# A transformer layer on one core: the last product moved into the next batch's slots, and the counting pass without its constant half

## The reference

```
x = L0_attn_x                                    # (16, 512, 256)
Q, K, V = heads(x @ Wq.T + bq), heads(x @ Wk.T + bk), heads(x @ Wv.T + bv)
scores = einsum('bhqd,bhkd->bhqk', Q, K) / 4     # (16, 16, 512, 512)
top_vals, _ = top_k(scores, 31)
scores = where(scores < top_vals[..., -1:], -inf, scores)
context = softmax(scores) @ V
x = layernorm(x + context @ Wo.T + bo)
gate, up = x @ (w_gate / 127).T, x @ (w_up / 127).T      # 768 hidden
x = layernorm(x + (silu(gate) * up) @ (w_down / 127).T)
```

## Time and profile before

| what | us |
|---|---|
| median of three runs (lowest, highest) | 2992.36 (2987.83, 2993.67) |
| the profiled execution's own time | 3002.92 |
| its span, from the first to the last instruction | 3001.1 |
| PE busy | 2705.3 (90%) |
| DVE, ACT, POOL busy | 2499.2, 2478.7, 2385.7 |
| mean granted TensorE clock | 0.959 of full speed |

### The profile page before, as it was taken

The page is one execution under the profiler, slowest core; times in us unless marked ns, Lnnn a source line. Parts: engine busy times, 40 slices in busy tenths (PEclk is TensorE's granted clock), DMA queues, the critical chain, the costliest instruction groups (busy, mean ns, idle before and its releaser), DMA issues.

```text
span 3001.1 us, 81706 instructions
## 1 busy us (share of the span) xinstructions
PE 2705.3 (90%) x21375; PEld 1449.9 (48%) x21375; DVE 2499.2 (83%) x12312; ACT 2478.7 (83%) x5890; POOL 2385.7 (79%) x1668
## 2 busy tenths in 40 slices
PE   5889999989998988899999999999988999899897
PEld 2444544545454444454545455454444545455455
DVE  5888888888889878888898988878888888888883
ACT  4888898888898877888888988878978888888883
POOL 1887888888798876787888888787877879778783
PEclk7899999999999989899999999999999999999998
DMA  3201111020111101111011110211101111110100
GB/s 88 48 21 42 25 41 38 24 49 26 37 30 36 42 21 37 29 29 45 23 42 25 41 39 24 47 27 37 30 25 45 26 40 27 32 42 23 37 2 22
DMA packets 91162, 102.67 MB, mean 34 GB/s; under 512 B 34529, under 2 KB 52962, under 8 KB 90594
## 3 DMA queue, kind: packets, MB, share of 16 engines
q1 hardware_dynamic: 89874, 96.35, 13.4%
q10 hardware_dynamic: 720, 0.14, 0.0%
HBM read 20.86 MB, written 8.39 MB: 10 GB/s over the span
## 4 chain that ended last, share of the span: by engine, by line
PE 36%; DVE 18%; SPq 15%; issue 13%; POOL 8%; ACT 6%; DMA 2%; DVEq 1%; ACTq 0%; POOLq 0%
SPq L386 8%; SPq L385 7%; DVE cand L941 7%; POOL mask L1219 6%; PE bench L740 5%; PE Y_ps L664 5%; PE ST_ps L684 4%; PE Y_ps L661 3%; PE ctxT_ps L698 3%; DVE S L934 3%; PE bench L734 3%; PE bench L605 3%; PE Y_ps L662 3%; PE ST_ps L681 3%; ACT junk L492 2%
## 5 line engine op out<-in xcount | busy, mean ns | idle before, releaser
L1219 POOL TENSOR_SCALAR mask<-S,thr,mb 128x512 bf16<-128x512 f32 x1015 | 2098.4, 2080 | 44.1 <-POOL mb L1213 33.5
L941 DVE MAX8 cand<-Y_ps 128x8 f32<-128x128 f32 x4096 | 1072.0, 282 | 7.4 <-issue 6.9
L492 ACT ACTIVATE junk<-S,at_zero,slope 128x512 bf16<-128x512 f32 x1024 | 824.7, 805 | 99.3 <-DVE S L934 99.2
L934 DVE TENSOR_SCALAR_CACHE_REDUCE S<-S_ps,na 128x512 f32<-128x512 f32 x1024 | 755.9, 738 | 170.7 <-PE S_ps L651 153.2
L502 ACT ACTIVATE above<-S,s,steep 128x512 bf16<-128x512 f32 x1024 | 824.6, 805 | 0.6
L510 ACT ACTIVATE PT<-ST_ps 128x512 f32<-128x512 f32 x1024 | 595.9, 582 | 193.0 <-PE ST_ps L684 187.4
L661 PE MATMUL Y_ps<-ones_b,nbig 128*128 128x512 bf16 x1024 | 403.0, 394 | 169.6 <-DVE cand L941 155.9
L651 PE MATMUL S_ps<-KS,QS 64*128 64x512 f32 x1024 | 523.0, 511 | 4.5 <-DVE S L934 2.3
L664 PE MATMUL Y_ps<-KS,QS 64*128 64x512 f32 x1024 | 523.0, 511 | 0.0
L684 PEld LDWEIGHTS ST_ps<-nbig,mask 128*128 128x128 bf16 x4096 | 235.8, 99 | 382.0 <-issue 382.0
L684 PE MATMUL ST_ps<-nbig,mask 128*128 128x128 bf16 x4096 | 414.8, 225 | 0.0
(11 more groups left out here) (187 smaller groups left out, 3684.6 us busy)
## 6 DMA issues: line engine op xcount, KB each, us to landing
QS<-Qhi SPq DMA_DIRECT2D x512, 32.0 KB, 2.0
KS<-Khi SPq DMA_DIRECT2D x512, 32.0 KB, 2.0
KS<-Klo SPq DMA_DIRECT2D x512, 32.0 KB, 2.0
QS<-Qlo SPq DMA_DIRECT2D x512, 32.0 KB, 2.0
xTs<-in_xT SPq DMA_DIRECT2D x17, 512.0 KB, 3.7
xs<-in_x SPq DMA_DIRECT2D x16, 512.0 KB, 3.9
out<-xs SPq DMA_DIRECT2D x15, 512.0 KB, 2.9
hT<-in_wgT SPq DMA_DIRECT2D x1, 768.0 KB
```

The source lines that it names most:

```text
L492: nc.scalar.activation(junk[:, :], S[:, score_place(j)[0], :], ACT.Tanh, bias=at_zero[:, :], scale=slope[:, hb, col:col + 1], accum_out=s0 ...
L934: nc.vector.tensor_scalar(S[:, at, :], S_ps[n % 2][:, :], na[:, hb, col:col + 1], None, ALU.add, op1=ALU.max, accum_out=rmax[:, n % RING:n ...
L941: mx = nc.vector.max(cand[:, j % CANDS, i, :], Y_ps[j % 2][:, i * BW:(i + 1) * BW])
L1219: nc.gpsimd.tensor_scalar(mask[:, h % MASKS, t, :], S[:, score_place(j)[0], :], thr[:, r:r + 1], mb[:, r:r + 1], ALU.is_lt, op1=ALU.add).t ...
```

## The change

Six things change together.

1. The four down products leave slots 59 to 62 and stand in slots 1, 2, 3 and 5 of the next batch, with DVE's sums and statistics one slot behind; the second layer norm is at slot 7 there, and the normalised rows at 10 and 12. Only batches from 2 on have them (`finish`), and the rest slots have the last ones.
2. Gate and up stand at 43/44, 46/47, 49/50, 52/53, 58/59 and 61/62. The products gram and quad go from 36 and 37 to 42 and 45, sums from 55 to 54.
3. `below` loses its constant product. ACT writes its Sign as one unsigned byte, the upper one of each bf16 of `above` (the lower stays 0): 1 gives 2^-125 and anything else 0. The weights are -2^127, so the product is 0 or -4. To match, W_k and b_k are multiplied by 2^-38 once, and the exponential's scale undoes it.
4. In 30 slots, the list `QUIET`, that product is made twice.
5. `flag` and `onesc` are bf16 (the small flag product is one pass, not two).
6. Batch 1 is written apart on all engines. The loops cover batches 2 to 15: seven batches per body on PE, ACT and POOL (one return, after batch 8), two on DVE (six returns, after batches 3, 5, 7, 9, 11 and 13).

```diff
-BIG = 2.0 ** 40
+SHIFT = 2.0 ** -38
+BIG = 4.0
+BYTE_BIG = 2.0 ** 127
...
-             26: "v", 31: "q", 33: "k", 35: "keys", 36: "gram", 37: "quad", 55: "sums"}
+             26: "v", 31: "q", 33: "k", 35: "keys", 42: "gram", 45: "quad", 54: "sums"}
...
-DOWN_SLOTS = {59: 0, 60: 1, 61: 2, 62: 3}
+DOWN_SLOTS = {1: 0, 2: 1, 3: 2, 5: 3}
...
-LN_SLOTS = {34: 0, 63: 1}
+LN1_SLOT, LN2_SLOT = 34, 7
...
-OUT_SLOTS = {1: (0, 1), 2: (2, 3)}
+OUT_SLOTS = {10: (0, 1), 12: (2, 3)}
...
-        if n in DOWN_SLOTS:
-            uses.append(("down", DOWN_SLOTS[n]))
+    if finish and n in DOWN_SLOTS:
+        uses.append(("down", DOWN_SLOTS[n]))
...
-TURN_OF, ACT_TURN_OF = 5, 7
+TURN_OF, DVE_TURN_OF = 7, 2
...
+QUIET = [n for n in range(TILES)
+         if all(what in ("flags", "keys", "gram", "quad") for what, _ in uses_of(n, False, False, True))]
...
-                nc.scalar.activation(above[:, j % 4, :], S[:, score_place(j)[0], :], ACT.Sign, bias=s0[:, j % 8:j % 8 + 1],
+                nc.scalar.activation(above[:, j % 4, :].bitcast(U8).rearrange("p (l y) -> p l y", y=2)[:, :, 1], S[:, score_place(j)[0], :], ACT.Sign, bias=s0[:, j % 8:j % 8 + 1],
...
-                nc.tensor.matmul(Y[:, :], nbig[:, :], ones_b[:, :], start=True, stop=False)
-                nc.tensor.matmul(Y[:, :], nbig[:, :], above[:, j % 4, :], start=False, stop=False)
+                for again in range(1 + (n in QUIET)):
+                    nc.tensor.matmul(Y[:, :], nbyte[:, :], above[:, j % 4, :], start=(again == 0), stop=False)
...
-                        pe.wait_ge(h_done, b * NF)
+                        pe.wait_ge(h_done, (b - 1) * NF)
                         mm = narrow(part)
...
-            with pe.Fori(1, B, TURN_OF) as b:
+            slots(1, False, False, False)
+            with pe.Fori(2, B, TURN_OF) as b:
                 for i in range(TURN_OF):
-                    slots(b + i, False, False)
-            slots(B, False, True)
+                    slots(b + i, False, False, True)
+            slots(B, False, True, True)
...
-            with dve.Fori(1, B, TURN_OF) as b:
-                for i in range(TURN_OF):
-                    slots(b + i, False, False)
-            slots(B, False, True)
+            slots(1, False, False, False)
+            with dve.Fori(2, B, DVE_TURN_OF) as b:
+                for i in range(DVE_TURN_OF):
+                    slots(b + i, False, False, True)
+            slots(B, False, True, True)
```

More of the change, by code:

```diff
@@ L742, in narrow, with on_bench @@
                 return mm
[L744 to L746 removed]
+            def on_bench(b, n, first, rest, finish):
+                for what, part in uses_of(n, first, rest, finish):
+                    use = place(b, n, what, part, first, rest, finish)
                     pe.wait_ge(taken, use)
```

116 lines of the change are left out of this document (62 added, 54 removed).

## The result

| | median of the runs, us | range | runs |
|---|---|---|---|
| before | 2992.21 | 2987.83 to 2993.67 | 4 |
| after | 3060.82 | 3056.57 to 3068.04 | 4 |

The ratio is 1.0234 with a 95% interval of [1.0208, 1.026]: the change makes the kernel 2.3% slower, about 70 us. The forecast was 3003 us with a range of 2955 to 3035. The direction was right, the size was not.

What follows compares the result with a forecast made beforehand. It took PE to bound slots 41 to 0 and ACT the light slots, with four engines close. Terms -153 + 120 + 10.8 - 4.5 + 30 + 8 = +11.3 gave 3003 us against the median, range 2955 to 3035.

Steps and rivals of the forecast that it cites:

- slots 41 to 0: Slot 41 to the next slot 0: bound goes from PE to ACT, 60.5 us, -10.2 each, -153 us in all.
- slots 1 to 5: Slots 1 to 5, batches 2 to 15: moved down products make them PE-bound at 19.9 us, +8.6 each, +120 us.
- rest slots: Rest slots after the last batch: its four down products find no cover on a busy PE, +10.8 us.
- slots 6 to 31: Slots 6 to 31: ten constant products go, but ACT and the load behind SP's issues hold the length, 0 us.
- slots 32 to 40: Slots 32 to 40: gram and quad leave while ACT is nearly full, -0.3 us each, -4.5 us.
- loop returns: DVE's loop returns, six instead of two: stall and half clock cost 7.6 us each, +30 us net.
- wait for the last hT: First down product in slot 1: PE waits for POOL's last hT, 1 us in eight batches, +8 us.
- the first rival: DVE's loop returns are cheap, one stop and no fall of the clock: -4 instead of +30, 2969 us; chance 0.22.
- The clock falls more often: PE with less work is granted half clock in more stretches: +50 us, or 3030 us if half count; chance 0.10.
- Everything comes through: ACT is not the bound, so the 7.5 us of constant products per batch are saved everywhere: 2925 us; chance 0.10.
- The late hT: PE stands in slot 1 for POOL's hT, 4 us in 14 batches: +48 at most, 3030 us; chance 0.16.

Runs made afterwards that it cites:

- b_down1: The kernel before with five of the six matmuls of each down product left out in the loop batches; 2931.97 us, ratio 0.9809.
- a_both7: The changed kernel with the fifth gate and up products at slots 59 and 60, sums at 51 and one DVE return; 3004.92 us, ratio 1.0051.
- b_bytes: The kernel before with the byte pass alone (no constant product, bf16 flags, W_k scaled), order and loops as before; 2992.84 us, ratio 1.0003.
- a_down_only: The changed kernel with gate, up, gram, quad and sums back in the slots of the kernel before; 3043.44 us, ratio 1.0162.
- a_gate59: The changed kernel with the fifth gate and up products one slot later (59 and 60), so slot 58 is free; 3036.94 us, ratio 1.0156.
- a_all_twice: The changed kernel with the byte product made twice in all 64 slots instead of 30; 3062.18 us, ratio 1.0234.
- b_bytes15: The kernel before with the byte pass alone and all fifteen batches in one loop body on PE, DVE and POOL; 2972.64 us, ratio 0.994.

## Why the prediction was wrong

Against the profiled execution, in us:

| term | forecast | measured | how |
|---|---|---|---|
| slots 41 to 0, without returns | -153 | -94 | -87.0, of which returns +7 |
| slots 1 to 5, without returns | +120 | +116 | +124.9, of which returns +9 |
| rest slots | +10.8 | +9.7 | what lies outside the batches' slots |
| slots 6 to 31 | 0 | -2 | table above |
| slots 32 to 40 | -4.5 | +8 | table above |
| loop returns | +30 | +16 | 6 x 5.3 less 16 |
| wait for the last hT | +8 | 0 | no such wait |
| sum | +11.3 | +53.7 | |

**The step that failed** is the first: "with short waits, as a near tie of three engines leaves them, I take 60.5 (ends 59.1 and 64). That is -10.2 each". Measured are 64.7 against 70.7, -6.0 each, outside even the upper end. This term alone is 59 us too low. The whole sum is only 42 short, since the other terms together were 17 us too high, the returns and the wait for hT above all: they hid part of the miss. ACT's busy time was right (59.05 forecast, 59.56 in batch 9). What failed is the step from a bound to a length. The runs show three things in its place:

- The bench wait of slot 58, an order effect that no busy time shows. Taking it away in two ways gave 23 and 30 us, some of it through the clock behind the returns. The forecast looked at what was removed from slots 59 to 62 and never asked what a product put into slot 58 would wait for: the bench's one bank, still holding the turned context.
- The down products were cover. Taking 132 us of them out of slots 59 to 62 saved 57 (`b_down1`). The forecast priced what leaves PE at its full length down to ACT's bound and called what stays short waits.
- ACT's bound is not reached. Even with both repairs (`a_both7`) slots 41 to 0 take 62.9 us by the medians, so that 1.8 of the 4.2 us by which 64.7 exceeds the forecast's 60.5 are gone and 2.4 stay; in batch 7 the stretch is 61.9 us with its fullest engine at 57.8, 93%. The light slots, where ACT was at 99 to 100%, were the wrong model for slots in which nearly every one has a product that passes over the bench. That it is the bench that makes the difference is likely from the waits above, and not shown: what holds these 2.4 us per batch stays open.

**Slots 1 to 5** were right: 20.2 us against a forecast of 19.9, PE full. So was the sentence that what was PE-bound with ACT idle stays so in another place; the stretches above are its measurement.

**Slots 32 to 40** went the other way, +8 for -4.5. Slots 38 to 40 grew, and nearly every batch after has a stretch at half clock from about slot 38 to 41, 3.4 to 13.7 us long. Over all batches slots 38 to 41 took 184 us before, 204 after, and 198 in `b_bytes`, so the byte pass alone can bring most of the growth. It does not always: `a_down_only` has it too, with gram and quad at 36 and 37 as before, and stands at 184. What else it takes is not shown.

**Loop returns** had the right mechanism and were mis-sized, 7.6 us each for 5.1 to 5.3. The stops are shorter (2.4 and 0.9 us for 3.3 and 1.8), as the first rival had said, though there are still two; the fall of the clock that it denied is there, 6.8 us after each. It costs 2.6 to 2.8 us in slots 1 to 5, where the forecast had 3.4. In `a_gate59`, without the wait of slot 58, the rival's price holds: no fall of the clock, and 1.8 to 2.6 us a return.

**The wait for the last hT** is absent: no row of PE's or PEld's waits names hT, and the down product in slot 1 starts straight behind the turned scores. POOL's side was right: the last hT of batch 8 is done 24.6 us after slot 57 begins (1643.29), 24 forecast.

```profile
1666.66 1.26 POOL L1272 TENSOR_TENSOR hT<-th,ups 128x512 f32<-128x512 f32 x1
```

PE's side was not: it reaches the down product at 1670.41, after 27.1 us and not 22 to 23, the wait of slot 58 among them.

**The rivals.** "The clock falls more often" was right as an observation (71 stretches for 36, 520 us for 250). As the cause of the 70 us it fails by `a_all_twice`, which is as slow with 285 us; behind the returns the fall does cost 2.6 to 2.8 us each. "Everything comes through" is refuted by `b_bytes`. The late hT did not occur. None of the rivals was an order effect on the bench. The range ended 26 us too low, since its slow cases, 3030 each, were a late hT and more falls of the clock at half their weight: the term's own upper end, 64, would have put 15 x 3.5 = 52 us on top of 3003 and was not among them. One count was off by one: eleven of slots 6 to 31 lose a constant product, not ten, which changes nothing at a term of 0.

What stays open: `a_both7` is 33 us above `b_bytes15` by the ratios. Over all batches the profiled executions place them, slots 1 to 5 +126 us, 6 to 31 +12, 41 to 0 -107, rest slots +9, but which single wait ends last in slots 41 to 0 was not isolated.

## What to carry to other kernels

Before a product is moved into a slot, ask what holds its buffer there, not only who is busy: one bank that is taken late cost a third of this change's loss, part of it not where the wait stood but at the next stop, where the clock fell again. Work taken from the bounding engine pays only down to where the others, which used it as cover, come up; take one piece out and measure before moving four. Moving a PE-bound piece from a stretch where the others idle into one where they are full moves the idle time with it.
